# Second weights side by side, and the low halves of Gelu's values last

## The reference, cut to what matters

```python
# first layer's experts, twice: stages moe0 and moe2; one expert per token, F = 256
h = jax.nn.gelu(xt @ W1[e], approximate=False) @ W2[e]
out = out + gate[:, None] * h
# second layer's experts, twice: stages moe3 and moe6; two experts per token, H = 512
h = jax.nn.gelu(jnp.einsum('bsd,dh->bsh', x, w1) + bb1, approximate=False)
y = jnp.einsum('bsh,hd->bsd', h, w2) + bb2
```

## Time and profile before

| | |
|---|---|
| median of 3 runs | 1114.45 us |
| the profiled execution's own time | 1116.47 us |
| its span, first to last instruction | 1114.7 us |
| TensorE matmul busy | 674.6 us (61%), granted clock 0.80 over the span |
| VectorE busy | 723.4 us (65%) |
| ScalarE busy | 524.2 us (47%) |
| GpSimd busy | 540.8 us (49%) |
| second product: lines 759, 760, 762 | 780 matmuls each |

### The profile page before, as it was taken

How to read it: one execution, slowest core, us unless ns; L and a number is a source line. 1 busy time by engine, 2 the same in 40 slices (tenths; PEclk the granted TensorE clock), 3 DMA queues, 4 the chain that set the end, 5 groups by cost and what they waited for, 6 DMA issues and landing times.

```text
span 1114.7 us, 20298 instructions
## 1 busy us (share of the span) xinstructions
PE 674.6 (61%) x5992; PEld 531.0 (48%) x5992; DVE 723.4 (65%) x2283; ACT 524.2 (47%) x1160; POOL 540.8 (49%) x562
## 2 busy tenths in 40 slices
PE   7115853589810586343899981488872569977900
PEld 7013531277710354343688870255552458766700
DVE  7884675989988355677355663599988636533542
ACT  3611333756550133251577871377762258755700
POOL 0007656586100562642676766465112656574475
PEclk9998985789955599555799995699885679988965
DMA  9602321000020133121233331111000123222242
GB/s 300 171 0 48 91 60 48 19 4 2 2 76 0 42 83 70 47 81 28 59 85 77 82 62 50 31 36 36 25 29 29 38 58 83 66 69 63 55 109 71
DMA packets 82502, 66.40 MB, mean 60 GB/s; under 512 B 10665, under 2 KB 74026, under 8 KB 82402
## 3 DMA queue, kind: packets, MB, share of 16 engines
q1 hardware_dynamic: 68674, 37.09, 11.5%
q0 software_dynamic: 13728, 28.02, 11.4%
HBM read 38.99 MB, written 26.08 MB: 58 GB/s over the span
## 4 chain that ended last, share of the span: by engine, by line
PE 24%; DVE 15%; issue 8%; another core or an unknown queue 6%; POOL 6%; ACT 3%; DMA 2%; DVEq 1%; POOLq 0%; ACTq 0%
POOL rt L1284 5%; PE bank L741 4%; PE bank L759 3%; PE bank L743 3%; PE bank L762 3%; PE bank L742 3%; PE bank L760 2%; DVE turned L1114 2%; PE bank L725 1%; DVE x L1172 1%; POOL ytok_loop L1284 1%; DVE arena L2025 1%; DMA rt<-y_moe,slot_i 1%; DVE arena L2018 1%
## 5 line engine op out<-in xcount | busy, mean ns | idle before, releaser
L1261 POOL DMA_INDIRECT turned<-xrows_moe,token x234 | 252.0, 1077 | 326.6 <-DVE token L1034 203.2
L1284 POOL DMA_INDIRECT rt<-y_moe,slot_i x176 | 174.9, 994 | 140.1 <-DVE x L1172 54.6
L817 ACT ACTIVATE turned<-bank,b1T 128x256 f32<-128x256 f32 (+1 forms) x372 | 131.5, 445 | 104.2 <-PE bank L743 47.1
L741 PE MATMUL bank<-rt,w1h 128*128 128x128 bf16 (+1 forms) x528 | 139.2, 264 | 27.9 <-issue 9.7
L759 PE MATMUL bank<-w2h,turned 128*128 x780 | 147.8, 224 | 10.0 <-issue 4.9
L760 PE MATMUL bank<-w2h,turned 128*128 x780 | 147.4, 224 | 9.8 <-issue 9.7
L1114 DVE TENSOR_TENSOR turned<-turned 128x1024 bf16<-128x1024 f32 (+1 forms) x119 | 127.3, 1070 | 34.0 <-ACT turned L822 19.0
L762 PE MATMUL bank<-w2l,turned 128*128 x780 | 133.8, 224 | 11.5 <-issue 10.9
L742 PE MATMUL bank<-rt,w1h 128*128 128x128 bf16 (+1 forms) x528 | 137.3, 261 | 1.7 <-issue 1.6
L743 PE MATMUL bank<-rt,w1l 128*128 128x128 bf16 (+1 forms) x528 | 137.0, 260 | 1.2 <-issue 1.2
L808 ACT ACTIVATE turned<-bank 128x512 f32<-128x512 f32 x40 | 24.0, 599 | 165.9 <-issue 86.4
(11 more groups left out here) (331 smaller groups left out, 1666.3 us busy)
## 6 DMA issues: line engine op xcount, KB each, us to landing
y_moe<-arena SPq DMA_DIRECT2D x119, 128.0 KB
xrows_moe<-xn SPq DMA_DIRECT2D x8, 512.0 KB
turned<-xrows_moe,token POOLq DMA_INDIRECT x234
rt<-y_moe,slot_i POOLq DMA_INDIRECT x176
x<-in_x SPq DMA_DIRECT2D x4, 512.0 KB, 5.9
arena<-in_w SPq DMA_DIRECT2D x1, 2048.0 KB, 9.6
xn<-in_w SPq DMA_DIRECT2D x8, 256.0 KB, 4.8
xrows_moe<-arena SPq DMA_DIRECT2D x4, 512.0 KB
```

The lines of the kernel that those rows point to most:

```text
L741: nc.tensor.matmul(o, wh, xh_t, start=True, stop=False)
L817: last = nc.scalar.activation(s["h32"][:, t % 2, o:o + width], bank[1 + 2 * (t % 2) + u // 2][:, at:at + width], ACT.Gelu, bias=b1T[:, ds( ...
L1261: nc.gpsimd.indirect_dma_start(out=s["xs"][:, 2 * (t % BODY) + j], out_offset=None, in_=s["xdram"], in_offset=bass.IndirectOffsetOnAxis(ap ...
L1284: nc.gpsimd.indirect_dma_start(out=brought_to(s, n), out_offset=None, in_=s["ydram"][0:P * UNITS] if s["halves"] == 2 and at < PART else s ...
```

## The change

The high and low halves of the second weights now lie side by side in one tile, `w2_0` or `w2_1`, 128 high columns and then 128 low columns for each block. `down` first takes all high halves of Gelu's values: each is loaded once, and 256 columns (high and low weights) stream past it into 256 columns of PSUM. After these it waits for "low", and then takes the low halves with the 128 high columns of the weights. A tile's result so stands in two parts of 128 columns in PSUM, and `finish` adds them: in the first layer with one reduction in place of the copy, in the second layer with one more addition, which waits (semaphore "biased") for the addition before it. The preparation of the weights writes to the new places.

```diff
-        w2h1, w2l1 = (sb(f"w2{h}1", [P, E, FC1, P], BF16) for h in "hl")
+        w2_1 = sb("w2_1s", [P, E, FC1, 2, P], BF16)
...
             def down(t, e):
...
-                y = [bank[5 + r][:, P * j:P * j + P] for j in range(2)]
-                w2hf, w2lf = (w[:].rearrange("p e c n -> p (e c n)") for w in (w2h, w2l))
+                both = [bank[5 + r][:, W * j:W * j + W] for j in range(2)]
+                y = [bank[5 + r][:, W * j:W * j + P] for j in range(2)]
+                w2f = w2[:].rearrange("p e c i n -> p (e c i n)").rearrange("p (a i) -> p a i", i=2)
                 pe.wait_ge(*s.at("y", t + 1))
+                pe.wait_ge(*s.at("act", t + 1 + RING))
+                halves = lambda name, u, j: s[name][:, k % 4, W * u + P * j:W * u + P * j + P]
+                weights_of = lambda u, j: w2f[:, ds((e[0] if s["pure"][t] else e[j]) + P * u, P)].rearrange("p a i -> p (a i)")
+                for u in range(FC):
+                    for j in js:
+                        nc.tensor.matmul(both[j], halves("hh", u, j), weights_of(u, j), start=(u + j == 0), stop=False)
                 pe.wait_ge(*s.at("low", t + 1 + RING))
                 for u in range(FC):
-                    hh, hl = ([s[n][:, k % 4, W * u + P * j:W * u + P * j + P] for j in range(2)] for n in ("hh", "hl16"))
-                    for group in (js,) if s["pure"][t] else [(j,) for j in js]:
-                        wh, wl = (w[:, ds(e[group[0]] + P * u, P)] for w in (w2hf, w2lf))
-                        for j in group:
-                            nc.tensor.matmul(y[j], hh[j], wh, start=(u + j == 0), stop=False)
-                            nc.tensor.matmul(y[j], hl[j], wh, start=False, stop=False)
-                        for j in group:
-                            last = nc.tensor.matmul(y[j], hh[j], wl, start=False, stop=(u == FC - 1 and j == js[-1]))
+                    for j in js:
+                        last = nc.tensor.matmul(y[j], halves("hl16", u, j), weights_of(u, j)[:, 0:P], start=False,
+                                                stop=(u == FC - 1 and j == js[-1]))
                 last.then_inc(s["down"], 1)
...
             def finish(t):
...
-                y = bank[5 + k % 2][:, 0:W].rearrange("p (j n) -> p j n", j=2)
+                y, ylow = (bank[5 + k % 2][:].rearrange("p (j i n) -> p j i n", j=2, i=2)[:, :, i] for i in range(2))
                 if s["bias"]:
...
+                    dve.wait_ge(*s.at("biased", t + 1))
+                    js = tiles_of(s["stage"], t)
+                    nc.vector.tensor_tensor(ysb[:, k % YRING, 0:js], ysb[:, k % YRING, 0:js], ylow[:, 0:js], ALU.add)\
+                        .then_inc(s["y"], 1)
                 else:
-                    nc.vector.tensor_copy(ysb[:, k % YRING], y).then_inc(s["y"], 1)
+                    js = tiles_of(s["stage"], t)
+                    nc.vector.tensor_reduce(ysb[:, k % YRING, 0:js], bank[5 + k % 2][:, 0:W * js].rearrange("p (j i n) -> p j n i", i=2, n=P),
+                                            AX, ALU.add).then_inc(s["y"], 1)
```

More of the change, by code:

```diff
@@ L115, in program @@
         w1h0, w1l0 = (sb(f"w1{h}0", [P, E, F0], BF16) for h in "hl")
-        w2h0, w2l0 = (sb(f"w2{h}0", [P, E, FC0, P], BF16) for h in "hl")
+        w2_0 = sb("w2_0s", [P, E, FC0, 2, P], BF16)
         w1h1, w1l1 = (sb(f"w1{h}1", [P, E, F1], BF16) for h in "hl")
-        w2h1, w2l1 = (sb(f"w2{h}1", [P, E, FC1, P], BF16) for h in "hl")
+        w2_1 = sb("w2_1s", [P, E, FC1, 2, P], BF16)
         wr = sb("wr", [P, 2, E])
@@ L149, in program @@
         spare = [w[:].rearrange("p a b -> p (a b)") for w in (w1h0, w1l0)] + \
-                [w[:].rearrange("p a b c -> p (a b c)") for w in (w2h0, w2l0)]
+                [w2_0[:, a:b].rearrange("p a b i c -> p (a b i c)") for a, b in ((0, E // 2), (E // 2, E))]
         x2n = spare[0].bitcast(F32).rearrange("p (k n f) -> p k n f", k=2, n=B)
@@ L243, in program @@
         splits = []
-        for st, hi, lo, loads in ((st_w1_1, w1h1, w1l1, ("w1", 16)), (st_w2_1, w2h1, w2l1, ("w1b", 16 * E))):
-            spec = "p a b -> p (a b)" if st is st_w1_1 else "p a b c -> p (a b c)"
-            splits.append((st, hi[:].rearrange(spec), lo[:].rearrange(spec), loads))
+        for st, hi, lo, loads in ((st_w1_1, w1h1, w1l1, ("w1", 16)), (st_w2_1, w2_1[:, :, :, 0], w2_1[:, :, :, 1], ("w1b", 16 * E))):
+            if st is st_w1_1:
+                part = lambda a, o: a.rearrange("p e f -> p (e f)")[:, o]
+            else:
+                part = lambda a, o: a.rearrange("p e c n -> p (e c) n")[:, o.start // P:o.stop // P]
+            splits.append((st, hi, lo, part, loads))
         PIECES = E * F1 // SPLIT
@@ L258, in cast, with like @@
                     o = slice(E // 2 * (i - 6), E // 2 * (i - 5))
-                    nc.scalar.activation(w2h0[:, o], st_w2_0[:, o], ACT.Copy).then_inc(pr["w0h"], 1)
+                    nc.scalar.activation(w2_0[:, o, :, 0], st_w2_0[:, o], ACT.Copy).then_inc(pr["w0h"], 1)
             return cast
+        def like(a, b):
+            return a if len(b.shape) == len(a.shape) else a.rearrange("p (c n) -> p c n", n=P)
         def split_high(act):
-            for st, hi, lo, (q, v) in splits:
+            for st, hi, lo, part, (q, v) in splits:
                 act.wait_ge(ld[q], v)
@@ L267, in split_high @@
                     o = slice(SPLIT * i, SPLIT * (i + 1))
-                    nc.scalar.activation(hi[:, o], st[:, o], ACT.Copy).then_inc(pr["w1h"], 1)
+                    h = part(hi, o)
+                    nc.scalar.activation(h, like(st[:, o], h), ACT.Copy).then_inc(pr["w1h"], 1)
         def split_low(dve, which):
-            st, hi, lo, loads = splits[which]
+            st, hi, lo, part, loads = splits[which]
             for i in range(PIECES):
@@ L275, in split_low @@
                 dve.wait_ge(pr["w1h"], PIECES * which + i + 1)
-                nc.vector.tensor_tensor(lo[:, o], st[:, o], hi[:, o], ALU.subtract).then_inc(pr["w1l"], 1)
+                h = part(hi, o)
+                nc.vector.tensor_tensor(part(lo, o), like(st[:, o], h), h, ALU.subtract).then_inc(pr["w1l"], 1)
         def rows_pool(pool):
@@ L622, in moe @@
                                        xhi=(2 - K) * (n // 2), onehot=2 * K,
-                                       inv=2 * K, idx=halves, half=(K - 1) * NT, turned=n // 2, up=n // 2, gelu=n // 2 * bias, comb=NT,
+                                       inv=2 * K, idx=halves, half=(K - 1) * NT, turned=n // 2, up=n // 2, gelu=n // 2 * bias, biased=n // 2 * bias, comb=NT,
                                        **{q: RINGS[q] + n // 2 for q in RINGS}))
@@ L690, in moe_tensor @@
                 last.then_inc(s["inv"], 1)
-            (w1h, w1l), (w2h, w2l) = s["w1"], s["w2"]
+            (w1h, w1l), w2 = s["w1"], s["w2"]
             pairs = s["pairs"]
@@ L1128, in finish @@
                     if s["pure"][t]:
-                        last = nc.vector.tensor_tensor(ysb[:, k % YRING], y, b2_all[:, ds(e[0], P)].unsqueeze(1).to_broadcast([P, 2, P]),
-                                                       ALU.add)
-                    else:
-                        for j in range(tiles_of(s["stage"], t)):
+                        nc.vector.tensor_tensor(ysb[:, k % YRING], y, b2_all[:, ds(e[0], P)].unsqueeze(1).to_broadcast([P, 2, P]),
+                                                ALU.add).then_inc(s["biased"], 1)
+                    else:
+                        js = tiles_of(s["stage"], t)
+                        for j in range(js):
                             last = nc.vector.tensor_tensor(ysb[:, k % YRING, j], y[:, j], b2_all[:, ds(e[j], P)], ALU.add)
-                    last.then_inc(s["y"], 1)
-                else:
-                    nc.vector.tensor_copy(ysb[:, k % YRING], y).then_inc(s["y"], 1)
+                        last.then_inc(s["biased"], 1)
+                    dve.wait_ge(*s.at("biased", t + 1))
+                    js = tiles_of(s["stage"], t)
+                    nc.vector.tensor_tensor(ysb[:, k % YRING, 0:js], ysb[:, k % YRING, 0:js], ylow[:, 0:js], ALU.add)\
+                        .then_inc(s["y"], 1)
+                else:
+                    js = tiles_of(s["stage"], t)
+                    nc.vector.tensor_reduce(ysb[:, k % YRING, 0:js], bank[5 + k % 2][:, 0:W * js].rearrange("p (j i n) -> p j n i", i=2, n=P),
+                                            AX, ALU.add).then_inc(s["y"], 1)
             packs = []
```

7 lines of the change are left out of this document (4 added, 3 removed).

## The result

| | us, median | range | ratio, 95% interval |
|---|---|---|---|
| before, 4 runs | 1113.91 | 1113.15 to 1115.78 | |
| changed, 4 runs | 1096.81 | 1095.99 to 1098.42 | 0.985, 0.983 to 0.986 |

The change makes the kernel 17.1 us faster. A repetition gave 0.984 (0.982 to 0.986), a third 0.985 (0.982 to 0.988).

A forecast was written before the change was run, and what follows sets the result against it. It took a loop through VectorE's finish, copy and `low`, the held gather and TensorE's signals as the bound. Its terms, +11.7 +3.2 +2.4 +1.3 -3.9, gave +14.7 us on the 1114.45 median: 1129.2 us, range 1103 to 1142.

The forecast's parts named there:

- in turns whose gather is held by `low`, all of it is passed on: Second-layer finish: the added addition's 0.45 us lengthens 26 turns (+11.7 us) and 7 in moe6's fetching part (+3.2 us).
- the loop: Turns of moe3, part of moe6: finish, copy, `low`, held gather, then TensorE's signals let through to the next finish; 3.24 us.
- the loop's own: VectorE's 1.35 us idle ahead of finish, claimed to belong to the loop; the argument against the addition being covered.
- in these turns TensorE waits: 3.24 us turns: TensorE alone needs 2.87 us, so it waits and the length of VectorE's finish counts in full.
- Mixed pairs: moe6's second product: a block takes 0.19 us for 0.22, 8 blocks in 16 pairs, -3.9 us, at most 7.
- The first layer: Finish there: a reduction over 512 numbers for a copy of 256, +0.2 us in 12 turns, +2.4 us.
- Pure pairs, second product: 1.34 us before, 1.33 after, as many columns as before: gain 0.
- The later wait: `down` may start before `low` has ended; claimed to win nothing in the 3.24 us turns: 0.
- Ends of stages: The last store waits for the last, longer finish: 2 x 0.45 + 2 x 0.2, +1.3 us.
- TensorE is what is late: Rival: the array really is behind, `down` needs less time after `low`, a turn wins 0.44 us; 1099 us, 16%.
- The gather slips out: Rival: the addition delays `low` past the second gather's start, so turns fall to 2.87 us; 1104 us, 12%.
- Covered: Rival: the 0.45 us goes into VectorE's idle time ahead of finish; 1112 to 1117 us, 14%.

The follow-up runs named there:

- Experiment 15: Kernel before, with the second layer's bias addition in finish done twice, the second behind a wait for the first; late signals: 1.002.
- experiment 18: Changed kernel with the second layer's `low` done in two operations of 128x512 in place of one of 128x1024; late signals: 0.989.
- experiment 16: Changed kernel; pure pairs without last addition, `low` waited for first, high x low left out, 16 matmuls of 128 columns: 0.983.
- experiment 8: Kernel before with the new second product and reduction in the first layer only, weights side by side everywhere; late signals: 0.998.
- 5: The changed kernel itself, measured again; late signals: 0.984 of the kernel before.
- 6: New second product and finish in mixed pairs of both layers only; pure pairs in the old order, weights side by side; late signals: 0.991.
- 13: Changed kernel with the wait for `low` put back ahead of all of `down` in pure pairs only; late signals: 0.986.
- 11: The changed kernel again, as yardstick beside 12, 13 and experiment 14; late signals: 0.985.
- 3: Kernel before with only the second product's order changed and `low` waited for later, narrow matmuls, no added addition; prompt signals: 0.999.
- 10: The kernel of 3 run again, also with prompt signals: 1.000.
- 7: Kernel before with only the weights side by side, a mixed pair's block taking both halves by one address; late signals: 1.002.
- 12: Kernel of 6, with pure pairs taking high halves first and waiting for `low` later, in narrow matmuls, no added addition; late signals: 0.989.
- experiment 14: Changed kernel without the last addition of finish in pure pairs; late signals: 0.986.

## Why the prediction was wrong

**The failed step** is "in turns whose gather is held by `low`, all of it is passed on" (+11.7 and +3.2 us). Its terms were right one by one: the addition costs 0.46 us, the gather ends 0.81 us after `low`, the signal comes after that. But I took a chain of events that follow one another in time for a loop of causes. Experiment 15 adds 0.45 us to the loop and two turns go from 6.48 to 6.53 us; experiment 18 shortens the held gather and turns stay at 3.1 to 3.3; experiment 16 takes 0.44 us off TensorE and they stay at 3.2. Three links, each shortened or lengthened alone, and none moved the pace. The rows did show the cover: 1.35 us of waiting ahead of finish, which I called "the loop's own". And "in these turns TensorE waits" misread the 0.4 us by which TensorE's turn was longer than 2.87: in most turns of the lock they are a stop inside the second product (1.70 us for 1.34 at 612.18). The addition does reach TensorE, whose first product starts right behind the copy, but what it costs there is nearly all won back by stops that no longer come: TensorE stands still for 13.5 us of moe3 in experiment 15 and 12.8 before.

**Mixed pairs** (-3.9 us): the mechanism was right, register work between narrow matmuls, the size was not. I took 0.19 us for 0.22 per block. Measured is 0.116 for a wide one and 0.056 for a low one, 0.17 a block: a block has one register instruction in place of two, it fits under the wide matmul, and the low matmuls have none. A pair takes 1.39 us for 1.92 (medians), and the 16 mixed pairs of moe6 give 5.8 to 6.8 us by the stages. My own upper bound, 7 us, was the better figure.

**The first layer** (+2.4 us) had the wrong sign: -3.7 us (moe0 and moe2 in experiment 8). The reduction takes 0.67 us for 0.42, as estimated. But all its pairs are mixed, and I counted the gain of the second product only in moe6, although the stages' list of pure and mixed pairs has all 40 of them.

**Pure pairs, second product** (0): this term was mis-sized most. The shortest second products take 1.32 for 1.34 us, as forecast; but 1.34 came from a turn without a stop (585.67), and in moe3 the mean was 1.54 before and is 1.34 now. These pairs bring 8.1 us (5 against 6). **The later wait** (0) was right, for late signals (13 against 11) and prompt ones (3, 10). **Ends of stages** (+1.3): with late signals the time after the last `low` went from 55.2 to 54.4, so it was no cost.

**The rivals.** "TensorE is what is late" has the nearest number, 1099, but by luck: its mechanism, less work between `low` and the "down" signal, falls with experiment 13. Its remark that TensorE itself is behind, and that wide matmuls may ease it, fits the stops. "The gather slips out", 1104, has one thing right: the addition breaks the lock. It gains next to nothing by that, and 71 gathers are still held, for 76. "Covered" is what happened to the addition; with a correct price for mixed pairs of both layers (-10 us) it would have given 1105 us.

**What stays open.** What delays TensorE's signals, whether its stops inside second products come of the same cause, and how much of the pure pairs' 8.1 us is those stops: in experiment 15 (24 narrow matmuls) only 6 of 35 are long, and moe3 takes 124.8 us all the same. Waits that the profile calls "remote", added up over all engines, are 265 us before and 254 to 278 in the five kernels with 24 narrow matmuls in a pure pair (6, 7, 8, 12, 15), 203 to 226 in seven of the eight executions with 8 or 16. The eighth is experiment 14, wide but in the lock, with 245. And in moe3 the "turned" signal is late by 1.1 to 1.4 us in the executions of the changed kernel (medians) where it was 1.6 before, "down" by 0.5 to 0.7 for 1.8 to 1.9. That fits a delay that grows with what TensorE issues, and doesn't prove it. I know of no version that beats the changed kernel: 12, 13, 14 and 18 are not faster.

## What to carry to other kernels

Events that follow one another to a hundredth of a microsecond can be a system in step and no loop of causes: before pricing an addition as passed on in full, look at the longest wait in the turn and ask who would really be late; and look inside the products of the engine that seems to wait, for stops that are no waits. Price short matmuls with register work among them by the block, the new form as well as the old, and for every stage that has them. Compare kernels only within one group of runs, and look first whether the kernel before takes the time there that its profile showed.

## What the runs showed of the hardware

The same kernel took 1013 or 1114 to 1122 us from one group of runs to the next. In the long groups TensorE's "turned" and "down" signals came 0.6 to 1.9 us late in the stages with indirect gathers (medians by stage, kernel before), and on time (0.01 us) between 204 and 366 us, where GpSimd has none; in the short groups they came after 0.01 us in moe3. In the lock of the kernel before TensorE also stopped for 0.2 to 0.4 us inside runs of 24 short matmuls, with no wait in the program there, and went on 0.15 to 0.23 us after the end of a held gather. Turns of moe3 took 3.2 to 3.4 us in the mean in all fourteen late executions, whatever was taken from or added to TensorE, VectorE or the held gather; with prompt signals 2.9. And a gather that started within a 128x1024 `low` ended 0.81 to 0.93 us after it (all 76 of the kernel before); one of the changed kernel that started within 0.02 us of the start of `low` wasn't held. A held gather gets on in the break before the next one: split in two, `low` held it until 0.8 us after its first half.
